# A batched attention kernel in fp32 on one core: transposes two steps behind the scores, value products between scores and transposes

## The reference

```python
xn = layernorm(x)                                   # over the 128 features
q, k, v = (einsum('bse,hde->bhsd', xn, W) + b ...)   # 16 heads of 64
scores = q @ k.T / 8, causal mask
att = softmax(scores) / 8
z = att @ v                                          # [16, 512, 64] per batch
attention = z.reshape(b, s, h * dh) @ proj           # NB: heads are not moved back beside dh
ffn = xn @ W.T + sum over 4 experts of gate * (xn @ Wd.T @ Wu.T)   # top-1 router, low rank
out = x + attention + ffn
```

## Time and profile before

| | us |
|---|---|
| median of 3 runs | 1349.98 |
| lowest and highest run | 1349.95, 1350.48 |
| the profiled execution | 1350.22 |
| its span, first to last instruction | 1348.5 |

### The profile page before, as it was taken

How to read it: one execution, slowest core, us unless ns; L and a number is a source line. 1 busy time by engine, 2 the same in 40 slices (tenths; PEclk the granted TensorE clock), 3 DMA queues, 4 the chain that set the end, 5 groups by cost and what they waited for, 6 DMA issues and landing times.

```text
span 1348.5 us, 34451 instructions
## 1 busy us (share of the span) xinstructions
PE 1330.6 (99%) x10783; PEld 1131.5 (84%) x10783; DVE 1106.3 (82%) x4001; ACT 1086.2 (81%) x3162; POOL 996.6 (74%) x1441
## 2 busy tenths in 40 slices
PE   6999999999999999999999999999999999999998
PEld 4788888888888888888888888888888888888887
DVE  7988888788887888878788787888878888788785
ACT  5887888888878887887888788788888887888785
POOL 6887776778767786777777768777677776778764
PEclk9999999999999999999999999999999999999999
DMA  5444544544545455444544444454455444545441
GB/s 152 105 106 117 116 111 103 129 108 103 122 107 127 95 117 121 108 114 107 123 106 114 120 105 110 118 118 112 101 120 119 103 119 113 122 96 118 117 104 48
DMA packets 112721, 150.85 MB, mean 112 GB/s; under 512 B 18271, under 2 KB 47262, under 8 KB 112542
## 3 DMA queue, kind: packets, MB, share of 16 engines
q1 hardware_dynamic: 111534, 148.30, 46.5%
q10 hardware_dynamic: 1008, 0.35, 0.1%
HBM read 10.69 MB, written 4.19 MB: 11 GB/s over the span
## 4 chain that ended last, share of the span: by engine, by line
PE 95%; ACT 1%; issue 0%; DVE 0%; DVEq 0%
PE zp L1314 22%; PE ptp L1290 20%; PE jobp L1160 13%; PE scores L1278 9%; PE scores L1281 7%; PE outp L1326 7%; PE jobp L1165 6%; PE scores L1259 4%; PE scores L1256 3%; PE jobp L1175 1%; PE outp L1335 1%; PE jobp L1180 1%; PE jobp L1351 0%; PE jobp L1170 0%; ACT prob L719 0%; PE outp L1340 0%
## 5 line engine op out<-in xcount | busy, mean ns | idle before, releaser
L630 POOL TENSOR_TENSOR prob<-prob,rden 128x128 f32<-128x128 f32 (+3 forms) x1024 | 712.7, 720 | 252.6 <-DVE rden L963 246.4
L974 DVE CUSTOM_DVE_ANT_0 prob<-scores,mask 128x128 f32<-128x128 f32 (+3 forms) x1024 | 471.4, 487 | 202.2 <-issue 131.8
L719 ACT ACTIVATE prob<-prob,nmax 128x128 f32<-128x128 f32 (+3 forms) x1024 | 567.5, 559 | 14.5 <-DVE nmax L974 8.0
L1290 PE MATMUL ptp<-ident,prob 128*128 128x128 f32 x2560 | 366.9, 274 | 2.2 <-ACT pt L730 1.8
L1290 PEld LDWEIGHTS ptp<-ident,prob 128*128 128x128 f32 x2560 | 295.0, 140 | 27.7 <-issue 3.7
L1314 PE MATMUL zp<-pt,v_sb 128*64 128x64 f32 (+3 forms) x4096 | 307.7, 303 | 0.0
L730 ACT ACTIVATE pt<-ptp 128x128 f32<-128x128 f32 (+3 forms) x512 | 221.1, 432 | 103.2 <-PE ptp L1290 103.2
L1314 PEld LDWEIGHTS zp<-pt,v_sb 128*64 128x64 f32 x4096 | 221.6, 137 | 51.2 <-issue 19.5
L986 DVE COPY pt<-ptp 128x128 f32<-128x128 f32 (+3 forms) x512 | 243.3, 475 | 3.7 <-PE ptp L1290 2.9
L573 POOL CAST k_low<-k_lo 64x512 fp32r<-64x512 f32 x256 | 156.0, 609 | 77.3 <-DVE k_lo L863 67.5
L1278 PE MATMUL scores<-k_twice,q_parts 128*128 128x384 f32 (+1 forms) x512 | 201.3, 393 | 0.8 <-DVE nmax L974 0.8
(11 more groups left out here) (191 smaller groups left out, 2001.9 us busy)
## 6 DMA issues: line engine op xcount, KB each, us to landing
k_twice<-k_hi SPq DMA_DIRECT2D x508, 128.0 KB, 2.3
q_parts<-q_lo SPq DMA_DIRECT2D x256, 128.0 KB, 2.4
q_parts<-q_hi SPq DMA_DIRECT2D x254, 128.0 KB, 2.3
xin<-in_L_attn_x_dram SPq DMA_DIRECT2D x16, 256.0 KB, 3.7
xres<-in_L_attn_x_dram SPq DMA_DIRECT2D x16, 256.0 KB, 3.0
out_dram<-osb SPq DMA_DIRECT2D x15, 256.0 KB, 2.6
pt<-in_L_attn_Wq_dram SPq DMA_DIRECT2D x1, 512.0 KB, 5.3
pt<-in_L_attn_Wk_dram SPq DMA_DIRECT2D x1, 512.0 KB, 6.1
```

The costliest lines, as they stand in the source:

```text
L630: nc.gpsimd.tensor_tensor(part, part, scale, ALU.mult).then_inc(pn_ready, 1)
L719: nc.scalar.activation(part, part, ACT.Exp, bias=nmax[:, s % NROT, h:h + 1], scale=-1.0, accum_out=den[:, s % NROT, h:h + 1]).then_inc(p_r ...
L974: nc.vector.tensor_tensor_reduce(out=prob[:, s % NROT, h, 0:cols], in0=scores[bank][:, first_col:first_col + cols], in1=mask[:, S - cols:S ...
L1290: done = nc.tensor.transpose(ptp[h][:, P * j:P * j + P], prob[:, s % NROT, h, P * j:P * j + P], ident[:])
```

## The change

Transposes come two steps behind the scores instead of three. Value products come six steps behind a pair's first unit instead of nine, so at steps with i = 2, and they stand between the scores and the transposes of that step. The z parts follow at lag 7 (i = 3) on ACT and DVE. Seven of the eight projection quarters of a batch are at steps with i = 1, ahead of the transposes there. DVE writes the low part of a key job at the end of the step with i = 2 (`subtracted`) instead of i = 1, that of a query job one step after the job as before. POOL's `pad_low_keys` for the key job of step s - 2 follows `normalise` of the step s with i = 2, and waits for that. One value job moves from step 22 to step 5. The router pieces, the layer norm statistics and the output sum move by one or more steps, most of them to steps with i = 2.

```diff
--- before.py
+++ after.py
@@ -69,10 +69,10 @@
 
 
 
-LAG_T = 3
-LAG_PV = (9, 9)
-LAG_Z, LAG_LOW_Z = 10, 11
-LAG_OUT = ((27, 31, 35, 39), (25, 27, 31, 35))
+LAG_T = 2
+LAG_PV = 6
+LAG_Z, LAG_LOW_Z = 7, 7
+LAG_OUT = ((25, 29, 33, 37), (25, 29, 33, 35))
 NROT = 4
 
 
@@ -84,7 +84,7 @@
 JOBS[1] = ("router", 0)
 JOBS[25] = ("xt", 0)
 JOBS[17] = ("gated", 0)
-V_STEPS = (29, 30, 2, 6, 10, 14, 18, 22)
+V_STEPS = (29, 30, 2, 5, 6, 10, 14, 18)
 for _n, _s in enumerate(V_STEPS):
     JOBS[_s] = ("v", _n)
 AHEAD = (25, 27, 28, 29, 30, 31)
@@ -96,14 +96,14 @@
 HI_KINDS = ("q", "k", "xt")
 
 STEP_ROUTER, STEP_GATED = 1, 17
-STEP_EVAC, STEP_BASE, STEP_OUT, STEP_FINAL, STEP_LORA = 20, 24, 21, 21, 24
-STEPS_STATS, STEP_AGGR, STEP_VAR = (5, 9), 17, 17
-STEP_RSTD, STEP_CENTRE, STEP_SCALE = 18, 19, 21
+STEP_EVAC, STEP_BASE, STEP_OUT, STEP_FINAL, STEP_LORA = 20, 24, 21, 22, 24
+STEPS_STATS, STEP_AGGR, STEP_VAR = (2, 6), 18, 18
+STEP_RSTD, STEP_CENTRE, STEP_SCALE = 19, 20, 22
 STEP_XRES = 28
-STEP_PRODUCTS, STEP_UNORM, STEP_EXPERTS = 3, 4, 7
+STEP_PRODUCTS, STEP_UNORM, STEP_EXPERTS = 3, 7, 9
 R_CHAIN = 14
-STEP_SPLIT, STEP_SUMMED, STEP_UP, STEP_BIAS_BANK, STEP_BIAS = (6, 10), 14, 13, 18, 21
-STEP_SUMS, STEP_LOGITS, STEP_WEIGHTS, STEP_FIRST, STEP_PARTS = 5, 6, 9, 10, 13
+STEP_SPLIT, STEP_SUMMED, STEP_UP, STEP_BIAS_BANK, STEP_BIAS = (6, 10), 14, 15, 18, 21
+STEP_SUMS, STEP_LOGITS, STEP_WEIGHTS, STEP_FIRST, STEP_PARTS = 6, 8, 10, 14, 14
 
 
 def bank_of(s):
@@ -115,6 +115,13 @@
     if s % NBLK == 1:
         return [s - 1, s]
     return [] if (s - 1) % NBLK == 1 else [s - 1]
+
+
+def subtracted(s):
+
+    if s % NBLK == 2:
+        return [s - 2]
+    return [] if s % NBLK == 3 else [s if s % NBLK == 1 else s - 1]
 
 
 def count_jobs(s, kinds=None):
@@ -565,7 +572,7 @@
 
                 n = JOBS[s][1]
                 made = c.fixed(c.job(s))
-                scaled = 0 if setup else c.fixed(c.head(s, 1))
+                scaled = 0 if setup else c.fixed(c.head(s + 2, 1))
                 if not setup:
                     pool.wait_ge(pn_ready, scaled)
                 pool.wait_ge(job_done[bank_of(s)], made)
@@ -653,8 +660,8 @@
                     if s == FIRST_X and not last:
                         low_inputs(c)
                     normalise(c, s)
-                    if s in JOBS and JOBS[s][0] == "k" and not (last and s in AHEAD):
-                        pad_low_keys(c, s)
+                    if s % NBLK == 2 and not (last and s - 2 in AHEAD):
+                        pad_low_keys(c, s - 2)
                     if b == 0 and s in STEP_SPLIT:
                         projection_parts(STEP_SPLIT.index(s))
                     if b == 0 and s == STEP_SUMMED:
@@ -805,8 +812,6 @@
                 cols = (slice(0, HALF), slice(HALF, S - P), slice(S - P, S))[o]
                 nc.scalar.activation(y_t[:, cols], outp[:, cols], ACT.Copy).then_inc(y_copied, 1)
 
-            evacuate_pt(c, -3)
-            evacuate_z(c, -2)
             evacuate_pt(c, -2)
             evacuate_pt(c, -1)
             evacuate_half(0)
@@ -1089,7 +1094,7 @@
                 router_late(c, s)
                 if s == 0 and not first:
                     job(c, UNITS - 1, back=1)
-                for js in evacuated(s):
+                for js in subtracted(s):
                     if js in JOBS and not (last and js in AHEAD):
                         job(c, js)
                 if s in STEPS_STATS and not last:
@@ -1130,9 +1135,7 @@
                                         xres[:].rearrange("p n e -> p (n e)")[:, cols], ALU.add).then_inc(final_ready, 1)
 
             reciprocals(c, -1)
-            evacuate_pt(c, -3)
             evacuate_pt(c, -2)
-            low_z(c, -2)
             evacuate_pt(c, -1)
             final_part(0, jobp[0], slice(0, HALF))
             low_z(c, -1)
@@ -1351,11 +1354,24 @@
                     done = nc.tensor.transpose(jobp[bank][:, cols], y_t[:, cols], ident[:])
                 done.then_inc(y_ready, 1)
 
+            def quarters(c, s, first, tail):
+                for o in range(NOCT):
+                    for quarter in range(4):
+                        n = due(s, OCT_STEPS * o + LAG_OUT[o][quarter], UNITS, first, tail)
+                        if n is not None:
+                            project(c, NOCT * n + o, quarter)
+
             def step(c, s, first=False, last=False, tail=False):
                 if not tail:
                     score(c, s, first)
                 if first and s == 0:
                     job(setup, LATER[2])
+                if s % NBLK == 1:
+                    quarters(c, s, first, tail)
+                p = due(s, LAG_PV, NBLK, first, tail)
+                if p is not None:
+                    for h in range(2):
+                        values(c, p, h)
                 unit = due(s, LAG_T, 1, first, tail)
                 if first and unit == 0:
                     pe.wait_ge(w_lo_ready, 5)
@@ -1365,15 +1381,8 @@
                     job(c, s)
                 if s == STEP_OUT and not first:
                     transpose_sum(c, tail)
-                for h in range(2):
-                    p = due(s, LAG_PV[h], NBLK, first, tail)
-                    if p is not None:
-                        values(c, p, h)
-                for o in range(NOCT):
-                    for quarter in range(4):
-                        n = due(s, OCT_STEPS * o + LAG_OUT[o][quarter], UNITS, first, tail)
-                        if n is not None:
-                            project(c, NOCT * n + o, quarter)
+                if s % NBLK != 1:
+                    quarters(c, s, first, tail)
                 if tail:
                     return
                 if first and s == STEP_BASE:
@@ -1416,11 +1425,8 @@
                                             start=False, stop=False, skip_group_check=True)
                 done.then_inc(o_ready, 1)
 
-            transpose(c, -3)
+            transpose(c, -2)
             project(c, -2, 2)
-            for h in range(2):
-                values(c, -2, h)
-            transpose(c, -2)
             transpose(c, -1)
             project(c, -2, 3)
             for h in range(2):
```

## The result

The changed kernel took 2019.64 us in the median of 4 runs (2012.20 to 2031.98), the kernel before 1350.16 (1349.95 to 1350.48): ratio 1.4966, 95% interval 1.4946 to 1.4986. It is slower, as forecast, but the forecast of 1898 is 122 us too low and the time lies outside the range of 1690 to 1970. The profiled run took 2012.2 us.

A forecast was written before the change was run, and what follows sets the result against it. PE, busy 99%, bounds the kernel at 82.47 us a batch. Waits less a small saving add 34.5 a batch, 552 for sixteen, less 4 in the last: 1350.2 + 548 = 1898 us, range 1690 to 1970.

The forecast's parts named there:

- Stall A: Next pair's first score matmul (S0) waits for POOL's casts of the padded keys: 4.64 us from S3, 21.4 a batch.
- Stall B: Value job at i = 2 waits for its bank until DVE has written `k_lo`: 1.40 us each, 8.4 a batch.
- Stall A longer at steps 22 and 26: Without a value job there, DVE's `k_lo` delays S3's maximum: 0.46 us each, about another 0.7 at 22.
- Sum of a batch: All waits less the saving add 34.5 us to each batch of 82.47 us.
- rival 3: TensorE's clock falls in the idle gaps: 1000 us more if throughout, about 2400 us at half of the pairs; chance 0.05.
- gap A: PE's idle gap before the next pair's first score matmul, forecast at 2.57 us in each pair.
- rows 12: Start-up stretch of the old trace: PE busy 3.06 of 5 us at clock 1.00, read as speaking against a clock loss.
- a clock below 1 would prove it wrong: Sign in the changed profile: the prediction is wrong if TensorE's granted clock is below 1.
- Saving of 0.05 a pair: On PE, transposes behind the value products pay less surcharge than score matmuls: 0.05 us a pair, 0.4 a batch.
- The transposes of unit 3 come two steps behind its scores ... 0.1 for each: PE's transposes of unit 3 wait for POOL's scaling, 2 x 1.04 us; counted as 0.1 us for each.
- Without stall B this would be late next: ACT's exponentials of unit 2 wait behind the copy of unit 0; estimated 1.7 us, covered by the wait for `k_lo`.
- Moving them back would give nothing: Statistics, z parts, SP's copies and input load in their new places cost nothing while the wait for the casts stands.

The follow-up runs named there:

- experiment 3: Changed kernel with POOL's two casts for the keys ahead of the scaling of unit 2 instead of behind it: 1710.23 us.
- experiment 5: Changed kernel with DVE's reciprocals of unit 2 ahead of the first maximum at i = 3 instead of behind it: 1780.57 us.
- experiment 4: Changed kernel with DVE writing the low part of the key job at i = 1 again: 1811.45 us.
- Experiment 2: Changed kernel with extra matmuls filling TensorE's idle gaps before each pair's first score matmul and before the value job: 1910.58 us.
- experiment 8: Kernel before with only the value products moved ahead of the transposes and job in their step, i = 1: 1430.68 us.
- experiment 7: Kernel before with only the transposes moved to two steps behind the scores instead of three: 1544.06 us.
- 9: Kernel before with value products ahead of transposes at i = 1, and ACT's exponentials and DVE's `k_lo` ahead of the copies: 1373.29 us.
- experiment 11: Changed kernel with casts first, exponentials and `k_lo` ahead of copies, reciprocals ahead of maxima, and DVE's copy of unit 1 behind both maxima: 1468.18 us.

## Why the prediction was wrong in size, point by point

- *Stall A, forecast 4.64 us from S3 to S0 and 21.4 a batch:* right. The median of the pairs that ran wholly at 2.4 GHz is 4.66 in the trace, experiment 3 removes it by moving the casts, and experiment 5 shows its least obvious link.
- *Stall B, forecast 1.57 from transposes to job (2.73 and 2.87 with a router piece):* right to 0.1 us, but for the last, which is 0.3 too long. Medians at full clock 1.48, 2.60 and 2.54; 95 waits forecast, 95 seen; experiment 4 removes it.
- *Stall A longer at steps 22 and 26 (0.46 + 0.7 and 0.46):* right. From S3 to S0 the medians there are 5.64 and 5.04 us.
- *Sum of a batch, forecast 82.4 + 34.5 = 116.9:* right. Adding up the full-clock medians of all the intervals between PE's pieces in one batch gives 116.88 us. PE's busy share was forecast at about 70% and reads 76%. Most of the difference is there at full clock too: PE counts as busy for 87.4 of the 116.9 us, 75%, where a batch of before has 82.4 us. The forecast took PE's busy time around waits as that of the dense stream.
- *The clock:* the step that failed. The prediction read PE busy 3.06 of 5 us at a clock of 1.00 in the start-up, took that as evidence that gaps do no harm, and gave the half clock no term in the sum, with rival 3 at 0.05 for the other case. That stretch holds one gap of 1.94 us, once. In the changed kernel gap A comes 127 times, 2.4 us in most, with another of 1.0 or 2.1 us close before it in 95 pairs. The clock falls at some of these pairs and not at others: at all 32 with the two long gaps, and at some with gap A alone, 12 of 32 here and 47 of 127 in experiment 4. So one quiet gap in rows 12 could not settle it. Rival 3 priced only large shares, the whole time (1000 us more) and half of the pairs (about 2400 us in all), and nothing smaller. 15% of the time came at half clock, which makes some 150 us by its rate. The true size: the intervals between PE's pieces that touch a half-clock stretch are longer by some 120 us in sum than the full-clock medians of the same intervals, and 2012 - 120 = 1892, beside the 1898 of the forecast. The runs of the changed kernel say nearly the same without any model: with the mean clock at 0.924 one took 2012.2 and at 0.909 another 2032.0, which is 64 us more at half clock for 20 us more time, 0.31 for each; 306 x 0.31 = 95. Experiment 2 then took the half clock away and 109 us with it. The statement in the prediction that a clock below 1 would prove it wrong was the right test. That the waits add up to 1898 so closely is in part luck. The links of the two stalls were each seen, but stall B was priced some 0.8 us a batch too high (0.09 at four steps, 0.13 and 0.33 at the two with router pieces), and something as large, which no run names, made up for it.
- *Saving of 0.05 a pair:* right in size (experiment 8), and without use. The order that earns it costs 80 us in the kernel before, 23 even with the queues rearranged. The rule in the Trainium skill, "TensorEngine Tiling (Array Packing)", section Tiling Modes, gives no saving; the 3.77 against 3.82 us speak for a small one. The surcharge that the prediction read from the chain view (0.37 against 0.18) is too large: by start distances the first score matmul behind value products takes 0.28, so it pays 0.10.
- *"The transposes of unit 3 come two steps behind its scores ... 0.1 for each":* harmless in the sum only because stall A stood there. Alone, with the orders of before, the shorter lag costs 194 us (experiment 7), about as much as taking stall B away gave back (208, experiment 4). So the prediction named the two waits that end last, and understated what stands behind them.
- *"Without stall B this would be late next" (exponentials behind the copies on ACT):* such a queue is what experiment 8 met, in the kernel before, and 9 shows it in numbers, together with `k_lo` on DVE. When stall B went in experiment 4, the wait of S0 on PE did not grow by it (297.0 us, against 304 in the change).
- *"Moving them back would give nothing" while stall A stands:* not tried alone. What the moved quarter and the later copies on SP cost once the stalls are gone is open, and so is the split of the last 118 us between experiment 11 and the kernel before. The waits of transposes for POOL (136.7 us on PEld, 38.2 on PE) are the largest left on PE, but the lag was not set back within the change.

## What to carry to other kernels

When a step is moved on a machine with in-order queues, follow each queue by itself: what now stands behind the moved instruction, and which independent work waits with it. A maximum ahead of a reciprocal, or a copy ahead of an exponential, was worth 239 and up to 57 us here, without any matmul moved. Once a forecast leaves TensorE idle by more than small amounts, give the clock a term of its own with a middle value, not only all or nothing, and do not take one quiet stretch of the old trace as proof that gaps are harmless: the same gap cost the clock in one pair and not in the next.

## What the runs showed of the hardware that was not expected

- More TensorE work made the kernel faster. 1741 extra matmuls in the idle gaps took the mean granted clock from 0.924 to 0.998 and the time from 2019.6 to 1910.6 us. The Trainium skill, "TensorE: Matmul & The Clock Gate", says that idle gaps between bursts bring the clock down and that keeping the engine busy holds it up. The runs agree in kind, with shorter gaps than the page warns of: a single one of 2.14 us in experiment 4, and 1.0 to 2.4 us close together in the change.
- How much the gaps cost the clock varies from run to run of the same program: its mean was 0.924, 0.919, 0.919 and 0.909, and the times follow in that order, from 2012 to 2032 us. Within one run gap A alone was followed by half clock in 47 of 127 pairs (experiment 4).
- Time at half clock cost less than half of its length, some 120 us for 306. The likely reason, not tested apart, is that part of such a stretch is a wait for other engines, which the slower matmuls use up.
